# The inverse of each chunk system kept row outermost, its expanded form group innermost

## What is computed

```
S  = S * exp(g_t)
kv = k_t . S
dv = (v_t - kv) * beta_t
S  = S + k_t (x) dv
o_t = q_t . S
```

## Time and profile before

| | |
|---|---|
| median of 3 runs | 6611.17 us (6609.73 to 6613.82) |
| the profiled execution | 6641.88 us, span 6640.2 us |
| busy DVE, PE, PEld | 4866.2 us, 4427.9 us, 3814.6 us |
| busy POOL, ACT | 3481.7 us, 3430.4 us |
| mean granted TensorE clock | 0.836 |
| the loop over halves | from about 241 us to 5971 us |

### The profile page before, as it was taken

One profiled execution on the slowest core, in us unless ns is written; L12 is line 12 of the kernel. 1 busy time (PEld: TensorE's weight loads), 2 busy tenths in 40 slices (PEclk: granted clock), 3 DMA queues, 4 the chain that ended last, 5 costly groups with the idle time before them and its releaser, 6 DMA issues. The chain is left out here.

```text
span 6640.2 us, 196141 instructions
## 1 busy us (share of the span) xinstructions
PE 4427.9 (67%) x78513; PEld 3814.6 (57%) x78513; DVE 4866.2 (73%) x9508; ACT 3430.4 (52%) x6010; POOL 3481.7 (52%) x2081
## 2 busy tenths in 40 slices
PE   1577666667666667666666766666766666655993
PEld 1566566566556666656555665665665665653662
DVE  3788888888888888888888888888888888860003
ACT  1555555565555555555556555555555555631220
POOL 3665555565555665555566555556655556632004
PEclk8788888888888888888888888888888888877996
DMA  2000000000000000000000000000000000012213
GB/s 93 2 6 6 6 6 6 6 6 3 5 6 6 6 6 6 6 6 6 6 6 6 3 5 5 6 6 6 6 6 6 6 6 5 4 46 102 73 59 108
DMA packets 77479, 109.71 MB, mean 17 GB/s; under 512 B 20576, under 2 KB 66208, under 8 KB 75424
## 3 DMA queue, kind: packets, MB, share of 16 engines
q1 hardware_dynamic: 67616, 71.42, 3.3%
q0 software_dynamic: 8960, 25.39, 1.3%
HBM read 57.89 MB, written 38.89 MB: 15 GB/s over the span
## 5 line engine op out<-in xcount | busy, mean ns | idle before, releaser
L1567 POOL TENSOR_TENSOR state<-state,gc_end 128x512 f32<-128x512 f32 x512 | 595.5, 1180 | 1635.1 <-PE bank L595 1577.9
L572 PE MATMUL bank<-state,ke 128*64 128x64 f32 x16384 | 650.2, 247 | 347.1 <-DVE outT L1288 188.2
L572 PEld LDWEIGHTS bank<-state,ke 128*64 128x64 f32 x16384 | 613.6, 160 | 420.5 <-issue 209.2
L608 PE MATMUL last_two<-dvs,kte 128*64 128x64 f32 x16384 | 681.5, 245 | 182.3 <-DVE dvs L1277 180.4
L589 PE MATMUL bank<-rhs,te 128*64 128x64 f32 x8192 | 410.3, 253 | 517.4 <-DVE rhs L1270 284.5
L847 ACT ACTIVATE ke<-kq 32x512 f32<-32x512 f32 x1024 | 643.0, 628 | 198.8 <-DVE kq L1202 185.1
L1251 DVE TENSOR_TENSOR last_two<-last_two,prod 128x31 f32<-128x31 f32 (+15 forms) x1984 | 692.5, 349 | 70.1
L608 PEld LDWEIGHTS last_two<-dvs,kte 128*64 128x64 f32 x16384 | 618.6, 158 | 199.5 <-DVE dvs L1277 187.7
L1249 DVE TENSOR_TENSOR prod<-bd,last_two 128x31 f32<-128x31 f32 (+15 forms) x1984 | 671.2, 338 | 68.3
L797 ACT ACTIVATE te<-tt 32x256 f32<-32x256 f32 x1024 | 422.0, 412 | 568.4 <-DVE tt L1254 557.8
L589 PEld LDWEIGHTS bank<-rhs,te 128*64 128x64 f32 x8192 | 343.4, 162 | 594.9 <-DVE rhs L1270 546.4
(11 more groups left out here) (256 smaller groups left out, 10538.6 us busy)
## 6 DMA issues: line engine op xcount, KB each, us to landing
w_sb<-in_L_ffn_W_dram SPq DMA_DIRECT2D x16, 1024.0 KB, 9.4
expert_rows<-ke SPq DMA_DIRECT2D x1, 8192.0 KB, 21.9
xrows<-expert_rows SPq DMA_DIRECT2D x16, 512.0 KB, 8.4
expert_outputs<-yrow POOLq DMA_DIRECT2D x16, 512.0 KB, 3.3
xt<-_attn_hidden_states_dram SPq DMA_DIRECT2D x32, 128.0 KB, 2.8
xr<-_attn_hidden_states_dram SPq DMA_DIRECT2D x32, 128.0 KB, 2.1
x_after_attention<-xr SPq DMA_DIRECT2D x32, 128.0 KB
xo<-x_after_attention SPq DMA_DIRECT2D x32, 128.0 KB
```

The costliest lines, as they stand in the source:

```text
L572: mm = pe.matmul(bank_mem[g][s, q % 4 * DK:q % 4 * DK + DK], ke[:, c, r, q, s], state[:, hh * HQ + q, r, :], start=(r == 0), stop=(r == 1))
L608: mm = pe.matmul(bank_upd[g][s, (q % 4) * P + r * DK:(q % 4) * P + r * DK + DK], kte[:, r, q, s], dvs[:, q, :], start=True, stop=True)
L1567: pool.tensor_tensor(sv, sv, gc_end[:, vh, 4 * g:4 * g + 4, c].unsqueeze(2).broadcast_to([P, 4, 2 * DK]), ALU.mult).then_inc(sem(f"state_f ...
```

## The change

`tt` changes from [chunk, group, row] to [row, chunk, group]. The transposing instruction L1254 then writes 1024 consecutive elements in a partition instead of runs with 32 elements between neighbours. `te` changes from [group, column] to [column, group]. ACT's copy writes 256 consecutive elements and reads 32 runs of 8, where it read 256 consecutive ones and wrote 8 runs of 32. TensorE's weights for a group are then the elements g, g+8, g+16, ..., that is 64 fp32 elements with 32 bytes between neighbours, where they were 64 consecutive ones. No instruction is added, removed or moved on any engine.

```diff
-        tt = sb("tt", [P, NC, HQ, C])
+        tt = sb("tt", [P, C, NC, HQ])
...
-        te = sb("te", [P, HQ, P])
+        te = sb("te", [P, P, HQ])
...
-                            pe.matmul(bank_mem[g][s, q % 4 * DK:q % 4 * DK + DK], te[:, q, s], rhs[:, q, :], start=True, stop=True)
+                            pe.matmul(bank_mem[g][s, q % 4 * DK:q % 4 * DK + DK], te[:, s, q], rhs[:, q, :], start=True, stop=True)
...
-                    ins = act.activation(te[s, :, 32 * m:32 * m + 32], tt[s, c, :, :], ACT.Copy)
+                    ins = act.activation(te[s, 32 * m:32 * m + 32, :], tt[s, :, c, :], ACT.Copy)
...
-                vec(dve.transpose(tt[:].rearrange("p c q i -> p i (c q)"), t_prob), "tt_ready", u + 1)
+                vec(dve.transpose(tt[:].rearrange("p i c q -> p i (c q)"), t_prob), "tt_ready", u + 1)
```

## The result

| | before | after |
|---|---|---|
| median of 5 runs on one chip | 6613.82 us (6609.73 to 6619.38) | 6645.9 us (6644.51 to 6647.05) |
| ratio to before, 95% interval | | 1.0051 [1.0037, 1.0064] |
| the profiled execution | 6641.88 us | 6646.36 us |

What follows compares the result with a forecast made beforehand. DVE's program was taken to set the pace. Slower weight loads (+68 us) less the shorter transpose (41.5 us) gave +26.5 us, a median of 6638; the forecast case spanned 6625 to 6650, the overall range 6562 to 6712.

Steps and rivals of the forecast that it cites:

- Part 1: DVE's transpose L1254: falls from 1894 to 1246 ns, 64 times, saving 41.5 us in full on the path.
- Rival D: L1254: the transpose doesn't get shorter; 6611 with TensorE hiding the stride, 6679 with the forecast's weight loads; chance 0.09.
- Part 2: ACT's copy into `te`: reading runs of 8 costs nothing, under 1 us either way, only chunk 0 exposed.
- rival B: TensorE's weight loads: ACT's price of 2.25 ns a column, net +95 us, 6706; chance with what lies between 0.10.
- Part 3: TensorE's strided weight loads: 1.77 ns a column, 0.94 us a block, +0.48 at full clock; 68 us in 64 halves.
- Rival A: TensorE's weight loads: the stride is hidden, 0.46 us a block, only the saving stays, 6570; chance 0.33.
- rival C: TensorE's weight loads: both array sides draw on one read, 1.81 us a block, net +365 us, 6976; chance 0.12.
- What reaches DVE: DVE's wait for TensorE: 0.96 us a half from chunk 1, 0.1 from chunk 0, none from covered chunks 2 and 3.

Runs made afterwards that it cites:

- e1: Changed kernel with `te` kept in pairs of groups, so TensorE's weights lie two by two, 8 bytes per pair: 6565.47 us, ratio to before 0.9926.
- e3: Changed kernel with only `tt` changed and `te` as before, so weights in order and ACT reading elements 128 bytes apart: 6600.83 us, ratio to before 0.9975.
- f1: e1 with a second buffer that puts weights 8 elements apart in chunk 1 alone: 6669.72 us, ratio to before 1.0051.
- f2: e1 with a second buffer that puts weights 8 elements apart in chunks 2 and 3 alone: 6637.37 us, ratio to before 1.0003.
- h3: Changed kernel with DVE's scan of the decays (L1143) two steps later in the solve: 6672.91 us, ratio to before 1.0060.
- h2: Kernel before the change with DVE's scan of the decays (L1143) two steps later in the solve: 6609.47 us, ratio to before 0.9962.
- e4: Changed kernel with only `te` changed and `tt` as before, so the transpose and ACT's copy write apart: 6743.43 us, ratio to before 1.0188.
- g1: e1 with the moving operand `rhs` kept as [column, group], its neighbours 32 bytes apart: 6678.94 us, ratio to before 1.0064, one run.

## Why the prediction was right

**Part 1, the transpose.** Right: 1250 ns against 1246 forecast from L1215, and on the path in full. The saving isn't fixed to a point in time: e1, which leaves nothing but this saving and clip and scan, is shorter by 49.3 us in the loop, some 41 of them here. The idle time of L1267 that no engine ends, at the loop's end, is 97.0 us in before and 96.8 in e1, so it moved along. Rival D falls with it.

**Part 2, ACT's copy.** Right. Runs of 8 cost nothing, and e3 shows that single elements would have cost 0.91 ns each. That is less than the 1.41 that I took from L893; at 32 elements L893 was a poor row for a price by the element. With 0.91, ACT comes to 1.76 ns, and rival B's 2.25 isn't borne out by the longer copy.

**Part 3, the weights.** The step that decides. I forecast 0.94 us for a block at the full clock from DVE's 1.77 ns; 0.94 was measured. Rival A (0.46), rival B (1.2) and rival C (1.8) are excluded by the timeline of after alone. The argument that decided between my forecast and A was that engines with different rates in order come to a like pace on elements apart; TensorE does so too, and at both of its clocks, 0.94 to 0.96 us. That it is the memory's pace stays an inference from these like prices; the jump between 8 and 16 bytes is what the runs show. The prediction gave rival A nearly the same chance, so the choice of side was a narrow one: a block costs 0.48 us more where 0.32 would have been even. Its upper bounds don't agree with its own working: columns at 1.9 ns come to some 6660, not to 6650.

**What reaches DVE.** 74.1 us against 68. Chunk 1 gave 0.98 us a half in the timeline and 0.99 in f1, forecast 0.96. Chunk 0 was forecast with 0.1 and gave 0.2. Besides rounding 0.12 down, the prediction left out at the half clock the 5 ns a load that it counted at the full one: with them a block is 0.94 us there too, 0.09 above the 0.85 of before and not 0.06. Measured are 0.94 and 0.96. No wait came at `dvs` in chunks 2 and 3.

**What I missed.** I took chunk 3 for covered because its `dvs` is, and didn't ask what stands behind it on TensorE. The grams do, and L1235 waits for them in any case. In after this is +9.7 us, in f2 +31.1. Nearly all of it comes in halves with a lower clock there. Windows of TensorE in before, at chunk 2 and at the end of chunk 3:

```profile
3059.00:3064.00 5.00, 4.44 (x84) 0.66 0.01 3
...
3070.00:3073.00 3.00, 2.06 (x64) 1.00 0.00 0
```

In after, at a chunk 3 at 1.2 GHz, the one of the timeline above, and at one at 2.4 GHz, with its first gram:

```profile
3089.00:3093.00 4.00, 3.77 (x66) 0.50 0.00 0
```

```profile
558.00:562.00 4.00, 3.45 (x92) 1.00 0.00 0
```

```profile
563.12 0.42 DVE L1235 TENSOR_TENSOR cos_t<-bank,bd 128x256 f32<-128x256 f32 x1 [1.28 <-PE bank L533]
```

In before the stretch at 1.2 GHz falls on the work behind chunk 2, which DVE doesn't wait for, and chunk 3 has 2.4 GHz in 55 of 63 halves. In after chunk 3 is partly at 1.2 in 31 of them, where the wait at the first gram is 1.67 us on average; in the other 32 it is 1.31, against 1.28 before. So of the 9.7 us about 8 come with the clock and under 2 from the longer blocks themselves. Why the stretch moved I haven't tried.

**The phase against POOL.** −7.6 us in clip and scan was nowhere in the sum. It made the total look better than its parts: without it the forecast of +26.5 would have met +42.8 in the loop. h3 against h2 gives 44 when the clip's 19.1 are taken off their 63.2. The time fell near the forecast partly because two omissions of opposite sign nearly cancel.

## What to carry to other kernels

TensorE's fp32 weights want at least two elements of one access in each 16 bytes; with one, a column takes about 1.8 ns, at 1.2 GHz as at 2.4. The moving operand costs about as much with its elements 32 bytes apart. Often half of a new layout is the gain: here pairs kept DVE's saving (−0.74%) and lost nothing on TensorE. When an engine's work gets longer under cover, ask what is queued behind it there and who waits for that, besides its own consumer, and look at the granted clock of that work in many repeats, not in one.

Small differences can be phase: an instruction of 0.3 or 0.4 us that ran beside one of POOL's took up to 1.9 or 2.3 here. Look at the groups whose work didn't change before a sum is called explained.

## What the runs showed of the hardware that was not expected

- Two fp32 weights on 16 bytes cost almost nothing (0.48 against 0.46 us a block), four elements apart the full price (0.94), and 8 or 16 apart no more.
- The weights read apart take nearly one time at both clocks: 0.94 us a block at 2.4 GHz, 0.94 to 0.96 at 1.2.
- With weights apart in chunks 2 and 3, more halves have part of chunk 3 at 1.2 GHz: 31 of 63 in after and 45 in f2, for 8 in before and 3 in e1. That goes with 0.4 to 0.7 us more of DVE's wait behind it in such a half; the slower loads as such add 0.03.
- Beside POOL the clip took up to 1.88 us for its 0.28, and the scan up to 2.25 for its 0.42, in before; every long one ended 0.08 and 0.28 us behind POOL's instruction.
- ACT, DVE and TensorE come to nearly one price for an fp32 element apart: 1.76 and 1.85 ns (e3, e4), 1.77 and 1.83 (L1240, g1) and 1.84 (after).
